# Token attention as one quadratic form with the value weights last, 48 down projections in split form, the opening by tiles, the router inside the actor's matrix

## The reference

```python
x = x + attn_a(layernorm(x), norm_weight, w_qkv, temperature, w_out)
x = x + ffn(layernorm(x), router_w, actor_w1, actor_b1, actor_w2, actor_b2, gate_w, up_w, down_w)
x = x + attn_b(layernorm(x), W_qkv, b_qkv, W_proj, b_proj)
x = x + ffn(layernorm(x), ...)                                  # the same weights again

def attn_a(x, ...):     # attention over channels: 8 heads of 16 channels, 512 tokens
    xn = x * rsqrt(mean(x * x) + 1e-6) * norm_weight
    q, k, v = heads(xn @ w_qkv.T)                # each (b, 8, 16, 512)
    q, k = l2norm(q) * exp(temperature), l2norm(k)
    return tokens(softmax(q @ k.T) @ v) @ w_out.T

def attn_b(x, ...):     # attention over tokens, one head of 128
    q, k, v = split(x @ W_qkv + b_qkv, 3)
    s = q @ k.T * 8 ** -0.5
    s = s * steps_of(sigmoid(s))                 # 2, 1.5, 1, 0.3 or 0.1 by band of sigmoid(s)
    return softmax(s) @ v @ W_proj + b_proj

def ffn(x, ...):        # 8 experts of 336 hidden channels, all computed, weighed by scores
    probs = softmax(x @ router_w.T)
    logits = clip(gelu(x @ actor_w1.T + actor_b1) @ actor_w2.T + actor_b2, -30, 30)
    k = argmax(logits) + 1
    scores = where(rank_of(probs) < k, probs, 0)
    return sum(scores[..., e] * ((silu(x @ gate_w[e].T) * (x @ up_w[e].T)) @ down_w[e].T) for e in range(8))
```

## Time and profile before

| | |
|---|---|
| median of 3 runs | 513.47 us (507.74 to 513.87) |
| the profiled execution | 508.82 us, its span 507.0 us |
| mean granted clock of TensorE | 0.997 |
| busy: TensorE / its weight loads | 490.1 / 350.5 us |
| busy: VectorE, ScalarE, POOL | 297.5, 247.6, 294.6 us |
| matmul records | 2152 |

### The profile page before, as it was taken

The page is one execution under the profiler, slowest core; times in us unless marked ns, Lnnn a source line. Parts: engine busy times, 40 slices in busy tenths (PEclk is TensorE's granted clock), DMA queues, the critical chain, the costliest instruction groups (busy, mean ns, idle before and its releaser), DMA issues.

```text
span 507.0 us, 6599 instructions
## 1 busy us (share of the span) xinstructions
PE 490.1 (97%) x2152; PEld 350.5 (69%) x2152; DVE 297.5 (59%) x705; ACT 247.6 (49%) x435; POOL 294.6 (58%) x306
## 2 busy tenths in 40 slices
PE   7798899999999999999999999999999999999997
PEld 6576666677676666767677677776767676666666
DVE  3647343746767795497844889459673443723332
ACT  3286637356725674238552387425671345223221
POOL 4344778348759393493564737546455555665554
PEclk9999899999999999999999999999999999999999
DMA  8600000000000000000000000000000000000000
GB/s 241 228 0 2 0 0 2 0 1 1 1 1 1 0 0 2 1 2 0 1 0 2 0 1 1 0 2 21 1 0 1 1 22 0 0 1 21 0 2 21
DMA packets 7933, 7.38 MB, mean 15 GB/s; under 512 B 732, under 2 KB 7772, under 8 KB 7900
## 3 DMA queue, kind: packets, MB, share of 16 engines
q1 hardware_dynamic: 7900, 6.97, 4.5%
HBM read 5.91 MB, written 1.05 MB: 14 GB/s over the span
## 4 chain that ended last, share of the span: by engine, by line
PE 74%; DVE 6%; ACT 3%; issue 2%; POOL 1%; DVEq 0%; ACTq 0%; POOLq 0%
PE bank L1150 23%; PE bank L1000 14%; PE bank L1002 13%; PE bank L1001 13%; PE bank L1201 3%; PE bank L1104 1%; DVE t L929 1%; PE bank L1189 1%; PE bank L1020 1%; POOL t L566 1%; PE bank L1158 1%; ACT sl L678 1%; ACT xn L582 1%; PE bank L1138 1%; PE bank L1112 1%
## 5 line engine op out<-in xcount | busy, mean ns | idle before, releaser
L566 POOL TENSOR_TENSOR t<-t,sl 128x512 f32<-128x512 f32 x105 | 136.2, 1301 | 111.2 <-DVE t L929 86.8
L678 ACT ACTIVATE sl<-bank 128x512 f32<-128x512 f32 x168 | 98.9, 595 | 161.3 <-PE bank L1002 151.6
L1150 PE MATMUL bank<-t,WD 128*128 128x512 f32 x328 | 161.6, 592 | 0.0
L929 DVE TENSOR_TENSOR t<-bank,sbc 128x512 f32<-128x512 f32 x105 | 72.2, 688 | 89.9 <-PE bank L1002 88.8
L1000 PE MATMUL bank<-xhF,WGh 128*128 128x512 f32 x168 | 98.9, 589 | 3.4 <-ACT sl L678 2.7
L566 POOL TENSOR_TENSOR t<-t,sbc 128x512 f32<-128x512 f32 x63 | 81.4, 1318 | 8.9 <-ACT sbc L672 8.0
L1150 PEld LDWEIGHTS bank<-t,WD 128*128 128x128 f32 x328 | 61.7, 188 | 28.6 <-issue 15.1
L929 DVE TENSOR_TENSOR t<-bank,sl 128x512 f32<-128x512 f32 x63 | 42.9, 685 | 55.7 <-ACT sl L678 25.2
L1000 PE MATMUL bank<-xhF,WUh 128*128 128x512 f32 x168 | 67.4, 401 | 1.4 <-DVE t L929 1.4
L1002 PE MATMUL bank<-xhF,WUl 128*128 128x512 f32 x168 | 66.6, 397 | 0.0
L1001 PE MATMUL bank<-xlF,WUh 128*128 128x512 f32 x168 | 66.5, 396 | 0.0
(11 more groups left out here) (184 smaller groups left out, 669.7 us busy)
## 6 DMA issues: line engine op xcount, KB each, us to landing
stage<-in_gate SPq DMA_DIRECT2D x7, 192.0 KB, 5.7
stage<-in_up SPq DMA_DIRECT2D x7, 192.0 KB, 6.0
WD<-in_down SPq DMA_DIRECT2D x7, 192.0 KB, 6.0
X<-in_x SPq DMA_DIRECT2D x4, 256.0 KB, 5.7
out<-X SPq DMA_DIRECT2D x3, 256.0 KB, 2.3
raw<-in_small SPq DMA_DIRECT2D x1, 388.0 KB, 5.3
out<-X SPq DMA_DIRECT2D x2, 128.0 KB, 1.9
raw<-in_small SPq DMA_DIRECT2D x1, 192.0 KB, 2.7
```

The costliest lines, as they stand in the source:

```text
L566: pool.tensor_tensor(t2[k % NT2][:, :], t2[k % NT2][:, :], by[:, :], ALU.mult).then_inc(a_done, 1)
L678: act.activation(sl[k % NSL][:, :], bank[k % 2][:, :], ACT.Silu).then_inc(silu_done, 1)
L929: dve.tensor_tensor(t2[k % NT2][:, :], bank[2 + k % 2][:, :], by[:, :], ALU.mult).then_inc(t2_done, 1)
L1150: pe.matmul(OACC[:, :], WD[:, c, :], t2[k % NT2][:, :], start=(c == 0), stop=(c == CH - 1 or k == TAIL[0] - 1))\
```

## The change

**Token attention.** With the centred and scaled rows x of a batch, q.k is written as one quadratic form x A x', where A is made once from the query and key weights and biases: `wqk` (two products with a centring matrix cen that POOL makes in `wc`) and `wa`. The last channel of x is replaced by ones (a centred row's last channel follows from the others), so biases are inside. `bqk` is then one projection z = A x instead of two, and `bs` multiplies z with the split x (xhS, xlS). P is applied to x itself, in xnB, as four products of 128x512 (`bo` 0 and 1), and the value weights come last: four products of 128x128 with wvp (`bw`), whose result is scaled and added to X in one step by `byx`. `bv` and `bvp` are gone.

**Down projections.** 48 of the 164 become split products. ScalarE copies `t2` to a rounded tile ah (`ah`, a ring of three), VectorE subtracts (`al`) into the same memory as t2, named t2r; WD is split once in seven pieces (`wd`: WDh on ScalarE, WDl on POOL). The planner chooses the groups in `halves`, where its estimates leave room: 31 to 33, 56, 57, 59, 81, 82, 98, 99, 101, 102, 119, 120, 122 to 125, 127 to 133, 135 and 142 to 163.

**Opening.** Products of batch 0 wait for single tiles of xn; the sums of squares go ahead of the product beside them, in a bank of their own; the first attention output is added and measured by tiles, from banks 0 to 3; the first xhF is copied in two halves, and the first gate product starts with its two parts that need only xhF; half of POOL's head mask is made before the first statistics.

**Router.** Its eight rows stand in columns 64 to 71 of the actor's matrix, so the three products of `route` give both; four transposes of 8 rows (`rt`) bring the logits to token-major form, and `rexp` and in part `rsum` are due one iteration later.

```diff
+SPLIT_FROM, WD_FROM = CH + 8, CH + 5
+NAH = 3
...
+R0 = 64
+C_ROUTER = C_ACTOR + R0
...
-           (8, "bqkl", 1), (11, "bs", 0), (11, "bsp", 0, 0), (12, "bsp", 0, 1), (12, "bsp", 0, 2), (13, "bsp", 0, 3),
...
-           (29, "bo", 0), (29, "bo", 1), (30, "bo", 2), (30, "bo", 3), (30, "byx")]
+           (28, "bo", 0), (29, "bo", 1), (30, "bw"), (30, "byx")]
...
+DVE_LOAD = dict(uk=.7, al=.9, stats=1.4, xl=.7, ar=.6, ascale=.5, amax=.6, awo=.5, y=.7, yT=.7, rt=.8, rsum=3.6, rrank=2.9,
+                gelu=1.7, actk=1.6, bv=.7, bsp=1.2, byx=2.4)
+DVE_ROOM, DEBT_ACT, POOL_LEAD = 0.7, 1.0, 1.5
...
+    def halves(k):
+
+        room = debt[0] < DEBT_ACT and dve_load[0] < DVE_ROOM + DVE_LOAD["uk"] and pool_free[0] < k + POOL_LEAD
+        for j in split:
+            if ("al", j) not in done and slot_of.get(("ah", j), last) < k:
+                add(("al", j))
+                debt[1] += COST["al"][2]
+        j = seen[0]
+        while j < len(um_end) and um_end[j] < k + 0.5 and slot_of["um", j] < k:
+            weights = slot_of.get(("wd", j % CH // WCH), last) + 1 < k
+            if j >= SPLIT_FROM and j not in TAIL and weights and room:
+                split.append(j)
+                add(("ah", j))
+                debt[0] += COST["ah"][1]
+            seen[0] += 1
+            if j in split:
+                break
+            j += 1
...
-                r.then_inc(consts_ready, 1)
+                return r
...
+            head_mask(range(H // 2))
...
+                if kind == "ah":
+                    k, i = s[1], split_at[s[1]]
+                    act.wait_ge(a_done, k + 1)
+                    if i >= NAH:
+                        act.wait_ge(down_done, split[i - NAH] + 1)
+                    act.activation(ah[i % NAH][:, :], t2[k % NT2][:, :], ACT.Copy).then_inc(ah_done, 1)
...
+                if kind == "al":
+                    k, i = s[1], split_at[s[1]]
+                    dve.wait_ge(ah_done, i + 1)
+                    dve.tensor_tensor(t2r[k % NT2][:, :], t2[k % NT2][:, :], ah[i % NAH][:, :].bitcast(F32),
+                                      ALU.subtract).then_inc(al_done, 1)
...
+                if kind == "bo" and s[2]:
+                    b = s[1]
+                    t = turn_of["bo", b, 0]
+                    wait_full(act, t)
+                    if b:
+                        wait_full(act, turn_of["bw", b - 1])
+                    act.activation(UT[:, :], m_bank(t)[:, :], ACT.Copy).then_inc(n_free(t), 1)
...
-                    for i in range(NT):
-                        a, o = slice(i * P, i * P + P), 3 * E * i
-                        pe.matmul(m[:, o:o + 2 * E], xh[:, a], router[:, :], start=True, stop=True)
-                        r = pe.matmul(m[:, o + 2 * E:o + 3 * E], xl[:, a], router[:, 0:E], start=True, stop=True)
+                    wh, wl = swide(1)
+                    three(m[:, :], wh, wl, xh[:, :], xl[:, :]).then_inc(m_full[t % 3], 1)
+                if kind == "rt":
...
+                    for i in range(NT):
+                        r = pe.transpose(m[:, i * E:i * E + E], xa[R0:R0 + E, i * P:i * P + P], ident[R0:R0 + E, R0:R0 + E])
...
+                    if k == 0:
+                        pe.wait_ge(xh_ready, split_no["F", 0] + 1)
+                        pe.matmul(bank[0][:, :], WGh[:, 0, :], xhF[0][:, :], start=True, stop=False)
+                        pe.matmul(bank[0][:, :], WGl[:, 0, :], xhF[0][:, :], start=False, stop=False)
...
+                    if k in split_at:
+                        i = split_at[k]
+                        r = three(OACC[:, :], WDh[:, c, :], WDl[:, c, :], ah[i % NAH][:, :], t2r[k % NT2][:, :],
+                                  start=(c == 0), stop=(c == CH - 1 or k == TAIL[0] - 1))
...
-                if kind == "bv":
...
-                    three(turn(t)[:, :], qh[:, a], ql[:, a], kh[:, :], kl[:, :]).then_inc(m_full[t % 3], 1)
+                    three(turn(t)[:, :], zh[:, a], zl[:, a], xhS[:, :], xlS[:, :]).then_inc(m_full[t % 3], 1)
...
-                        r = pe.matmul(m[:, a], PT[:, j, a], v[:, j, :], start=(j == 0), stop=(j == NT - 1))
+                        r = pe.matmul(m[:, :], xnB[b % 2][:, j, :], PT[:, j, :], start=(j == 0), stop=(j == NT - 1))
...
+                if kind == "bw":
...
+                        r = pe.matmul(m[:, a], UT[:, a], wvp[:, :], start=True, stop=True)
```

More of the change, by code:

```diff
@@ L145, in needs @@
     if kind in ("xT", "xl") and s[1] == "B":
-        return [("bv", prev)]
+        return [("bs", prev, NT - 1)]
+    if kind == "xn" and s[1] == "B":
+        return [("bo", b - 2, 1)]
     if kind == "bo":
-        return [("bpT", b, i) for i in range(NT)]
+        return [("bpT", b, i) for i in range(2 * s[2] + 2)] + [("byx", prev)]
     if kind == "yT":
@@ L177, in plan, with bank_free @@
     um_end, downs, block_end = [], [0], []
+    split, seen = [], [0]
+    dve_load = [0.0]
+    slot_of = {}
+    wds = [("wd", j) for j in range(CH // WCH)]
+    def bank_free(by):
+        return by in done and (by[0] != "byx" or slot_of[by] < k)
     def ready(s):
@@ L221, in products @@
             j = downs[0]
-            if j < len(um_end) and um_end[j] + AFTER_POOL <= k and (j % CH or j == 0 or block_end[j // CH - 1] + OACC_REST < k):
+            if j in split:
+                due = slot_of.get(("al", j), last) < k
+            else:
+                due = j < seen[0] and um_end[j] + AFTER_POOL <= k
+            if due and (j % CH or j == 0 or block_end[j // CH - 1] + OACC_REST < k):
                 add(("down", j))
@@ L241, in plan @@
                 th[0] -= th[0] <= k
+        halves(k)
         products(k, 2)
+        if wds and k >= WD_FROM and k % 2:
+            add(wds.pop(0))
+            debt[0] += 0.5
         pe = 2.2
@@ L262, in plan @@
         debt = [max(0.0, act - pe), max(0.0, dve - pe)]
-    assert not any(th[1] for th in threads)
+        dve_load[0] = max(0.0, dve_load[0] - pe)
+    assert not any(th[1] for th in threads) and not wds
     while downs[0] < last:
@@ L281, in build @@
     xT_turn = {norm_no[s[1:]]: turn_of[s] for s in steps if s[0] == "xT"}
+    split = [s[1] for s in steps if s[0] == "ah"]
+    split_at = {k: i for i, k in enumerate(split)}
     split_no = {s[1:]: i for i, s in enumerate(s for s in steps if s[0] == "xT" and s[1] != "A")}
@@ L312, in build @@
         rows = sb("rows", [P, 272])
-        bq = sb("bq", [P, 1])
+        cen, last, qT, kT, wa = (sb(n, [P, P]) for n in ("cen", "last", "qT", "kT", "wa"))
         wbT, wvp = sb("wbT", [P, P]), sb("wvp", [P, P])
@@ L329, in build @@
         nmrs = [sb(f"nmr{i}", [P, NT]) for i in range(2)]
-        router = sb("router", [P, 2 * E], F32R)
-        logits = sb("logits", [P, NT, E])
         pe_ = sb("pe_", [P, NT, E])
@@ L347, in build @@
         sl = [sb(f"sl{i}", [P, T]) for i in range(NSL)]
+        t2_at = cursor[0]
         t2 = [sb(f"t2{i}", [P, T]) for i in range(NT2)]
+        cursor[0] = t2_at
+        t2r = [sb(f"t2r{i}", [P, T], F32R) for i in range(NT2)]
+        WDh, WDl = (sb(n, [P, CH, P], F32R) for n in ("WDh", "WDl"))
+        ah = [sb(f"ah{i}", [P, T], F32R) for i in range(NAH)]
         xaT = [sb(f"xaT{i}", [P, T]) for i in range(2)]
@@ L548, in _ @@
                     pool.wait_ge(factor_ready, s[1] + 1)
-                    pool.tensor_tensor(hq[:, :], hq[:, :], xa[:, :], ALU.mult).then_inc(inner_ready, 1)
+                    pool.tensor_tensor(hq[:, :], hq[:, :], xa[0:AH, :], ALU.mult).then_inc(inner_ready, 1)
+                if kind == "wc":
+                    chain(pool.memset(last[:, :], 0.0))
+                    pool.tensor_copy(last[:, P - 1:P], ident[:, P - 1:P])
+                    chain(pool.memset(cen[:, :], 0.0))
+                    chain(pool.affine_select(out=cen[:, :], in_=cen[:, :], compare_op=ALU.not_equal, fill=-1.0,
+                                             base=1 - P, pattern=[[0, P]], channel_multiplier=1))
+                    pool.tensor_tensor(cen[:, :], cen[:, :], ident[:, :], ALU.add).then_inc(cen_ready, 1)
                 if kind == "wp":
@@ L554, in _ @@
                     pool.tensor_tensor(lo, stage[j][:, :], hi.bitcast(F32), ALU.subtract).then_inc(wl_pool, 1)
+                if kind == "wd":
+                    at = slice(WCH * s[1], WCH * s[1] + WCH)
+                    pool.wait_ge(wdh_ready, s[1] + 1)
+                    pool.tensor_tensor(WDl[:, at, :], WD[:, at, :], WDh[:, at, :].bitcast(F32), ALU.subtract).then_inc(wdl_ready, 1)
                 if kind == "um":
@@ L587, in _ @@
                     t = turn_of[s]
+                    if (what, b) == ("F", 0):
+                        act.wait_ge(half_full, 1)
+                        act.activation(xhF[0][:, 0:T // 2], bank[3][:, 0:T // 2], ACT.Copy).then_inc(xh_half, 1)
                     wait_full(act, t)
@@ L1123, in _ @@
                         pe.wait_ge(silu_done, k - 1)
-                    three(bank[k % 2][:, :], WGh[:, c, :], WGl[:, c, :], xh, xl).then_inc(g_full, 1)
```

(5 more changed lines are left out.)

347 lines of the change are left out of this document (202 added, 145 removed).

## The result

Timed side by side, the changed kernel takes 507.01 us (median, 505.49 to 511.44), the kernel before 510.14 (507.74 to 513.87): ratio 0.9941, 95% interval 0.9914 to 0.9968. That is 0.6% faster where 3% were forecast, and 1.0 us above the forecast's range of 489 to 506. The profiled execution took 505.80 us, its span is 504.0.

What follows compares the result with a forecast made beforehand. TensorE, busy 97% of the span, was taken as the bound. Terms -15.2, -3.1 and +3.5 sum to -14.8, from 508.8 to 494.0 us, placed 1.5 higher at 495.5; range 489 to 506.

Steps and rivals of the forecast that it cites:

- TensorE's work, -15.2: Products removed, added or made cheaper on TensorE, summed part by part: 15.2 us less work.
- Router: Four transposes of 8 rows a block replace eight small products: 0.43 us instead of 0.91, -3.8 us over 8 blocks.
- The hole of the earlier trace: TensorE's 1.67 us wait for a silu ending at 52.88: costed at 0, bounds -1.5 and +2.
- The opening, -3.1: Four edits on the chain before the first gate product: 3.1 us saved, bounds -0.5 and -4.
- Rival 2: The opening gives nothing back, taken by a ScalarE hole and a second half-clock spell: 498.8 us, chance 0.13.
- Seven weight pieces: Copies on ScalarE and subtractions on POOL beside iterations 27 to 39: costed at nothing, as no split product waits before iteration 46.
- New waits of TensorE +3.5: TensorE's added waiting, as much again as its present 3 us plus 0.45 in batch 0: +3.5 us, bounds 0 and +12.
- `al` about 1.4 for the 26 others: VectorE's subtraction outside the last loop takes about 1.4 us each beside POOL's products, 36 us in all.
- The copy's wait for POOL's product is covered: ScalarE's copy `ah` waits for POOL's 1.30 us product, hidden because `down` comes three iterations after its t2.
- Rival 1: Attention stages turn VectorE-bound; 26 splits earn nothing and their `al` adds 0.3 us each: 505.8 us, chance 0.14.
- Rival 4: POOL's product wins the port lock each time in the last loop, making VectorE too slow: 524 us, chance 0.04.
- The trace agrees: One VectorE comparison, 0.28 us alone and 2.13 beside two POOL products, was read as confirming the exclusive port lock rule.

Runs made afterwards that it cites:

- f4: The changed kernel with the opening of the kernel before, no work by tiles ahead of the first gate product: 509.56 us, ratio 1.0002.
- f2: e1's order with the change's 48 splits and seven weight pieces set into it, nothing else moved: 496.36 us, ratio 0.9753.
- e1: The changed kernel with no split down products and no weight pieces, the rest of the change kept: 497.03 us, ratio 0.9759.
- f3: The changed kernel with the seven weight pieces made but no down product split: 503.60 us, ratio 0.9893.
- f1: The changed kernel's order with halves, low parts and weight pieces taken out, all down products plain: 504.52 us, ratio 0.9913.
- g1: The changed kernel with the weight pieces' GpSimd cost left out of the planner's table: 506.29 us, ratio 0.9928.
- g3: f2 with each low part ahead of VectorE's up product instead of behind it: 493.16 us, ratio 0.9674.
- e4: The changed kernel with the router's transposes of batch 2 one iteration later: 503.46 us, ratio 0.9888.
- e3: The changed kernel with three token products put ahead of the fifth norm's statistics on GpSimd: 503.40 us, ratio 0.9885.
- e2: The changed kernel with only the 22 down products of the last stretch split: 494.68 us, ratio 0.9703.
- h1: g1 with the last weight piece moved behind the attention's step of iteration 39: 498.71 us, ratio 0.9806.

## Why the prediction was wrong

- **TensorE's work, -15.2: right** (-15.8). Loop of the last stretch forecast 2.10, measured 2.09. P times V: two products from 203.89 to 205.61, 0.86 each, as forecast. Router: 4 transposes of 8 rows from 169.39 to 169.73, 0.34 where I took 0.43 (the earlier trace rows had 0.91 for what went). The hole of the earlier trace rows stayed, 1.40 us before the gate product at 50.79, as costed.
- **The opening, -3.1: right** (-2.6 at the first gate product, 2.5 to 3.1 us at the end by f4). Rival 2, that it gives nothing back, is out.
- **Seven weight pieces "costed at nothing": the step that failed.** Their own time was hidden in f2: it is no slower than e1, and the rest in block 1, where they stand, is no larger. But I asked only who waits for them, and they were priced in the planner's table; f3 and f1 show that this moved the token attention and cost 6.6 to 7.5 us. Nor is a piece always hidden: in g1 the last one closed the gap on GpSimd, and TensorE waited 6.6 us. I had the changed order before me and read it at the places of the new steps, not for the old ones that had moved.
- **"New waits of TensorE +3.5": the term that was mis-sized, for it left out the order.** 15.1 came, over its upper bound of 12. By the rest in each trace (9.6 in e1, 17.8 in f1, 26.4 in the change, 11.3 before) 8.2 are the order's and 8.6 the splits' in that order, less 1.7 that the other edits took away. In e1's order the same splits add 5.9 (f2).
- **"`al` about 1.4 for the 26 others": wrong, 0.79** (0.74 in the mean over all 48, the longest 1.77). The forecast named the port pair and took VectorE as the payer. Mostly GpSimd paid: its product rose from 1301 to 1450 ns, and the 41 products that begin beside a running low part take 1.68 us in the mean. The rows that show both, and ScalarE's half:

```profile
L634 POOL TENSOR_TENSOR t<-t,sl 128x512 f32<-128x512 f32 x105 | 151.8, 1450 | 93.2 <-DVE t L1052 70.6 <-ACT sl L757 22.5
...
L1060 DVE TENSOR_TENSOR t2r<-t,ah 128x512 fp32r<-128x512 f32 x48 | 35.6, 741 | 2.8 <-ACT ah L767 2.8
...
L767 ACT ACTIVATE ah<-t 128x512 fp32r<-128x512 f32 x48 | 30.2, 628 | 15.2 <-POOL t L634 14.0 <-PE bank L1113 0.9
```

- **"The copy's wait for POOL's product is covered": wrong by 14 us of ScalarE's time**, in the third row. It becomes TensorE's wait only where a silu is queued behind.
- **Rival 1 has the right number, 505.8, for another reason.** It wanted VectorE as the bound by the length of `al`. A stage where VectorE has no room there is, but TensorE does not stop for it:

```profile
233.00:252.40 19.40, 19.40 (x72) 12.61 (x71) 18.98 (x38) 14.92 (x25) 10.88 (x11) 1.00 0.00 0
```

VectorE is busy 98% of these 19.4 us and TensorE all of them; e1, at 497 us and without an `al`, has as full a stage (19.02 us from 168.0). That the early splits earn nothing held in the change and nearly in f2, but much of it is one place in VectorE's queue, since g3 gets 3 to 4 us back with a longer `al`.
- **The rivals lacked the one that came**: a step that costs nothing by itself, in a planner's input, moves others into collisions. Rival 4 (lock in the last loop) was excluded as forecast: `al` goes first there.
- **"The trace agrees in the earlier trace rows" was too short.** The rule quoted beside it has the waiting operation stand back for one instruction; the earlier trace rows has the comparison wait through two products. That was the sign of what g1 showed.

What stays open: most of the order's waits were summed and not followed back one by one, so why these steps collide there is argued for the ones above only. The half-clock stretches come with some waits and not with others of like length (TensorE waited 1.40 us at 39.43 in the change, ahead of a stretch from 42.2; 1.39 us at 39.24 in e1, and none followed; in e4, whose edit comes later, none either), and no run moved one alone.

## What to carry to other kernels

Where a planner or a scheduler sets the order, a new step's price in its table is part of the change: compare the places of the old steps first, and run the new order without the new work. When a gain has gone, do both halves, new order with old work and old order with new work; here that took two kernels. A step that feeds TensorE through VectorE belongs ahead of what has slack, even if it then runs longer beside GpSimd.

## What the runs showed of the hardware

A VectorE operation with both inputs in SBUF can wait for a whole train of GpSimd products, where the earlier trace rows had shown 2.13 us beside two: 7.52 us for `ge<-ge,tri` in g1 (0.28 alone), 4.22 in e3 and 4.21 in f3. In e2 it is `gt<-pr`, which took 1.49 us at the same place in e1; behind it TensorE waits 3.7 us:

```profile
124.35 6.33 DVE L1005 TENSOR_TENSOR gt<-pr 128x256 bf16<-128x256 f32 x1
...
125.47 4.93 POOL L634 TENSOR_TENSOR t<-t,sbc 128x512 f32<-128x512 f32 x4
```

But it need not wait so long. The same comparison in e3 and in the change, each begun while a product of a train runs:

```profile
185.28 8.70 POOL L639 TENSOR_TENSOR t<-t,sbc 128x512 f32<-128x512 f32 x7
...
189.90 4.22 DVE L1015 TENSOR_TENSOR ge<-ge,tri 128x256 bf16<-128x256 bf16 x1
```

```profile
184.13 6.34 POOL L634 TENSOR_TENSOR t<-t,sbc 128x512 f32<-128x512 f32 x5
...
188.76 0.57 DVE L1010 TENSOR_TENSOR ge<-ge,tri 128x256 bf16<-128x256 bf16 x1
```

In e3 it starts 0.36 us before the running product ends and waits for three more. In the change it starts 0.38 us before, and is done 0.19 us after, while the train goes on. Nothing here tells what decides between the two. The seven executions of e2 lie in two groups, four at 493.2 to 494.7 us and three, with the traced one, at 499.2 to 500.6; that the 6.33 us make this difference is not shown. A gap in the train ends the wait: in f2 and h1 the comparison takes 0.43 and 0.42.

The Trainium skill, page "SBUF — State Buffer", section "SBUF: two separate sides", has the lock as going to whoever starts first, for one instruction. The long rows go further, since the waiting operation also lost the turns between products; in the change it got the first. The other way round the price is small: in the last stretch a low part that starts first adds 0.38 us to the product beside it (1.68 against 1.30).
